# A post-LN decoder block with recurrent layers: other load order and other engines for the weight preparation ahead of the first step

## What is computed

```
for l in range(4):
    x = x + slstm(ln(x) * ln1_w[l], conv_w[l], conv_b[l], wi, wf, wz, wo, rker, cell_b, gn_w)[l]
    x = x + (gelu(u[..., :336]) * u[..., 336:]) @ ff_down[l],   u = ln(x) * ln2_w[l] @ ff_up[l]
x = ln(x) * post_w
```

## Time and profile before

| | us |
|---|---|
| median of 3 runs | 3654.46 (3654.07 to 3657.61) |
| profiled execution | 3654.35, its span 3652.6 |
| mean granted PE clock | 0.988 of full |
| PE / VectorE / ScalarE / GpSimd busy in the first 46 us | 11.0 / 33.4 / 1.3 / 1.6 |
| busy over the whole span, same order | 3518.5 / 3414.1 / 3045.7 / 2311.6 |

### The profile page before, as it was taken

The page is one execution under the profiler, slowest core; times in us unless marked ns, Lnnn a source line. Parts: engine busy times, 40 slices in busy tenths (PEclk is TensorE's granted clock), DMA queues, the critical chain, the costliest instruction groups (busy, mean ns, idle before and its releaser), DMA issues. The chain is left out here.

```text
span 3652.6 us, 168847 instructions
## 1 busy us (share of the span) xinstructions
PE 3518.5 (96%) x71457; PEld 2338.8 (64%) x71489; DVE 3414.1 (93%) x9400; ACT 3045.7 (83%) x6636; POOL 2311.6 (63%) x2515
## 2 busy tenths in 40 slices
PE   5999999999999999999999977999999999999997
PEld 3666666666666666666666654666666666666665
DVE  8999999999999999999999987999999999999997
ACT  4999999999999999999999965767776767777775
POOL 3777777777777777777777737555555555555552
PEclk9999999999999999999999998999999999999998
DMA  2000222000011010111001100000000000000000
GB/s 83 26 25 26 57 60 56 26 26 26 25 26 27 26 26 26 26 27 26 25 26 25 27 28 18 25 25 25 25 25 25 27 30 28 25 25 25 24 8 10
DMA packets 99980, 104.35 MB, mean 29 GB/s; under 512 B 17296, under 2 KB 95004, under 8 KB 98728
## 3 DMA queue, kind: packets, MB, share of 16 engines
q1 hardware_dynamic: 99224, 93.56, 9.0%
HBM read 48.52 MB, written 17.53 MB: 18 GB/s over the span
## 5 line engine op out<-in xcount | busy, mean ns | idle before, releaser
L572 POOL TENSOR_TENSOR conv_products<-normed_features,conv_taps_by_token 128x256 f32<-128x256 f32 (+1 forms) x837 | 758.2, 921 | 597.7 <-ACT normed_features L355 419.6
L299 PE MATMUL banks<-up_centred,after_cell_features 128*32 128x336 f32 x8928 | 684.2, 446 | 4.0 <-DVE after_cell L534 3.7
L783 POOL TENSOR_TENSOR exps_of_both_halves<-scores 128x256 f32<-128x256 f32 x512 | 404.5, 815 | 427.3 <-ACT scores L1062 424.8
L299 PEld LDWEIGHTS banks<-up_centred,after_cell_features 128*32 128x32 f32 x8928 | 302.2, 109 | 299.8 <-issue 245.6
L306 PE MATMUL banks<-down,hidden_features 112*32 112x256 f32 x6696 | 420.8, 383 | 0.2
L1062 ACT ACTIVATE scores<-scores 128x512 f32<-128x512 f32 x512 | 302.8, 624 | 81.4 <-DVE scores L1213 81.4
L394 ACT ACT_TABLE_LOAD x279 | 358.0, 1283 | 4.9
L373 ACT ACT_TABLE_LOAD x279 | 358.0, 1283 | 4.9
L585 POOL TENSOR_TENSOR conv_partial_sums<-conv_products,conv_partial_sums 128x512 f32<-128x512 f32 x279 | 358.4, 1284 | 0.0
L1213 DVE SCALAR_TENSOR_TENSOR scores<-banks,score_top 128x512 f32<-128x512 f32 x512 | 317.3, 681 | 6.4 <-PE banks L888 3.0
L273 PE MATMUL banks<-recurrent_weights,h_features 64*32 64x256 f32 x8928 | 313.8, 380 | 0.0
(11 more groups left out here) (224 smaller groups left out, 9946.5 us busy)
## 6 DMA issues: line engine op xcount, KB each, us to landing
layer_inputs<-layer_outputs SPq DMA_DIRECT2D x279, 96.0 KB, 2.1
layer_inputs<-in_x SPq DMA_DIRECT2D x280, 32.0 KB, 1.8
x_scratch<-layer_outputs SPq DMA_DIRECT2D x279, 32.0 KB, 2.1
x_tokens<-in_x SPq DMA_DIRECT2D x32, 256.0 KB, 3.1
context_features<-in_ctx SPq DMA_DIRECT2D x32, 256.0 KB, 3.7
layers_out<-x_scratch SPq DMA_DIRECT2D x32, 256.0 KB, 2.8
out<-result SPq DMA_DIRECT2D x64, 128.0 KB, 1.8
up_centred<-in_ff_up SPq DMA_DIRECT2D x1, 2688.0 KB
```

Of the source, the lines that this page charges most:

```text
L299: mm = nc.tensor.matmul(bank[group(l), b, 0:UP], xmt[:, n, group(l)], up[:, l, n, at:at + UP], start=n == 0, stop=n == HALF - 1, skip_grou ...
L572: return nc.gpsimd.tensor_tensor(prod[:, i:i + n], xnt[:, j % NRING].rearrange("p n t -> p (n t)")[:, None, :].broadcast_to([P, n, HALF * ...
L783: nc.gpsimd.tensor_tensor(psum[:, i % RING, :], pr[:, i % RING, 0:S], pr[:, i % RING, S:2 * S], ALU.add).then_inc(halves_added, 1)
```

## The change

- SP issues the bias rows first, then ln2, ln1, taps, conv bias and gn_w, then `up`, then gate and recurrent weights, then `down`. Each group has a semaphore: `rows_loaded`, `small_loaded` (5 loads), `up_loaded`, `gates_loaded` (2), `down_loaded`. PE waits for the last of these ahead of the down product of step 0.
- `up` is scaled by ScalarE, eight activations with the function Identity and a scale for each partition.
- PE waits for each layer's two scaled halves and signals the means of each layer; VectorE subtracts layer by layer.
- 14 of the memsets go to GpSimd, which signals `zeroed` after each (`CLEARED` = 14), and so do the ten fills of partial sums. `mean_w` is set first on VectorE.
- VectorE's order becomes: remaining memsets, bias, centre, taps and `gnc`, `bn_stats`, then the gate weights, then the subtraction.

```diff
         def _(sy):
-            for dst, src in ((wg, a["gate_w"]), (rk, a["rker"]), (up, a["ff_up"]), (down, a["ff_down"]), (conv_w, a["conv_w"]), (conv_b, a["conv_b"]),
-                             (ln1, a["ln1"]), (ln2, a["ln2"]), (gnc, a["gn_w"]), (rows, a["bias"])):
-                sy.dma_start(dst[:], src).then_inc(w_loaded, DMA)
+            sy.dma_start(rows[:], a["bias"]).then_inc(rows_loaded, DMA)
+            for dst, src in ((ln2, a["ln2"]), (ln1, a["ln1"]), (conv_w, a["conv_w"]), (conv_b, a["conv_b"]), (gnc, a["gn_w"])):
+                sy.dma_start(dst[:], src).then_inc(small_loaded, DMA)
+            sy.dma_start(up[:], a["ff_up"]).then_inc(up_loaded, DMA)
+            for dst, src in ((wg, a["gate_w"]), (rk, a["rker"])):
+                sy.dma_start(dst[:], src).then_inc(gates_loaded, DMA)
+            sy.dma_start(down[:], a["ff_down"]).then_inc(down_loaded, DMA)
             sy.wait_ge(zeroed, 1)
...
-            pe.wait_ge(w_step, UP_SCALED)
+            pe.wait_ge(mean_made, 1)
             for l in range(LAYERS):
+                pe.wait_ge(up_scaled, HALF * (l + 1))
                 for m in range(2):
                     for n in range(HALF):
...
-            mm.then_inc(up_means, 1)
+                mm.then_inc(up_means, 1)
...
+                if j == 0:
+                    pe.wait_ge(down_loaded, DMA)
                 feed_down().then_inc(down_done, 1)
...
+            act.wait_ge(small_loaded, SMALL * DMA)
+            act.wait_ge(up_loaded, DMA)
+            for l in range(LAYERS):
+                for m in range(HALF):
+                    nc.scalar.activation(up[:, l, m, :], up[:, l, m, :], ACT.Identity, scale=ln2[:, l, m:m + 1]).then_inc(up_scaled, 1)
             act.wait_ge(first_gates, 1)
...
+            nc.vector.memset(mean_w[:], 1.0 / D).then_inc(mean_made, 1)
             n = 0
-            for buf, val in ((xr, 0.0), (h, 0.0), (half_r, 0.0), (ls, NEVER), (dl, 0.0), (xm, 0.0), (xst, 0.0), (prod, 0.0), (hid, 0.0),
-                             (hidt, 0.0), (xnt, 0.0), (xmt, 0.0), (gl, 0.0), (xn, 0.0), (stat2, 0.0), (rstd, 0.0), (eps, EPS), (bias, 0.0), (pick16, 0.0),
-                             (mean_w, 1.0 / D), (begun, 0.25 * H_SCALE), (never, 0.0)):
+            for buf, val in ((bias, 0.0), (pick16, 0.0), (stat2, 0.0), (rstd, 0.0), (eps, EPS), (begun, 0.25 * H_SCALE), (never, 0.0)):
...
-            dve.wait_ge(w_loaded, DMA * LOADS)
...
+            dve.wait_ge(rows_loaded, DMA)
             f_ = rows[:, 0:1024].rearrange("p (h g d) -> p h g d", h=HEADS, g=GATES)[:, :, 1, :]
...
+            for r in (0, 64):
+                nc.vector.tensor_scalar(centre[r:r + DH, :], ident[r:r + DH, r:r + DH], -1.0 / DH, None, ALU.add).then_inc(w_step, 1)
+            dve.wait_ge(small_loaded, SMALL * DMA)
...
+            dve.wait_ge(zeroed, CLEARED)
+            nc.vector.bn_stats(stat2[:], xm[:, 0]).then_inc(w_step, 1)
+            n += 1
+            dve.wait_ge(gates_loaded, 2 * DMA)
             for l in range(LAYERS):
+                for m in range(HALF):
+                    w_ = wg[:, l, m, 2:4, :].rearrange("p g d -> p (g d)")
+                    nc.vector.tensor_scalar(w_, w_, ln1[:, l, m:m + 1], None, ALU.mult).then_inc(w_step, 1)
...
+            for l in range(LAYERS):
+                dve.wait_ge(up_means, l + 1)
                 for m in range(HALF):
                     w_ = up[:, l, m, :].rearrange("p (k n) -> p k n", k=2)
                     nc.vector.tensor_tensor(w_, w_, bank[:, 2 * l:2 * l + 2, 0:UP], ALU.subtract).then_inc(w_step, 1)
...
             dve.wait_ge(bias_made, 10)
+            dve.wait_ge(parts_made, 2 * (TAPS + 1))
             dve.sem_inc(w_ready, 1)
...
+            for buf, val in ((xr, 0.0), (xm, 0.0), (h, 0.0), (half_r, 0.0), (ls, NEVER), (dl, 0.0), (xst, 0.0), (prod, 0.0), (hid, 0.0),
+                             (hidt, 0.0), (xnt, 0.0), (xmt, 0.0), (gl, 0.0), (xn, 0.0)):
+                nc.gpsimd.memset(buf[:], val).then_inc(zeroed, 1)
+            pool.wait_ge(small_loaded, SMALL * DMA)
+            for turn_ in range(2):
+                for k in range(TAPS + 1):
+                    b_ = conv_b[:].rearrange("p l n -> p n l")
+                    nc.gpsimd.tensor_scalar(part[:, turn_, k].rearrange("p (n l b) -> p n l b", n=HALF, l=LAYERS),
+                                            b_[:, :, :, None].broadcast_to([P, HALF, LAYERS, B]), 0.5, None, ALU.mult).then_inc(parts_made, 1)
             pool.wait_ge(w_ready, 1)
```

More of the change, by code:

```diff
@@ L32 @@
 ROW_SCALE = 16.0
-UP_SCALED = 39
 EPS = 1e-5
@@ L222, in group @@
         return slice(32 * l, 32 * l + 32)
-    LOADS = 10
+    SMALL, CLEARED = 5, 14
     FIRST_PIECE = 40
@@ L420, in _ @@
-            dve.wait_ge(const_made, 4)
[L421 to L426, removed]
@@ L436, in _ @@
-            n += 1
-            for k in range(TAPS):
-                w_ = conv_w[:, :, :, TAPS - 1 - k].rearrange("p l n -> p n l")
-                nc.vector.tensor_copy(taps[:, k], w_[:, :, :, None].broadcast_to([P, HALF, LAYERS, B])).then_inc(w_step, 1)
-            for turn_ in range(2):
-                for k in range(TAPS + 1):
-                    b_ = conv_b[:].rearrange("p l n -> p n l")
-                    nc.vector.tensor_scalar(part[:, turn_, k].rearrange("p (n l b) -> p n l b", n=HALF, l=LAYERS),
-                                            b_[:, :, :, None].broadcast_to([P, HALF, LAYERS, B]), 0.5, None, ALU.mult).then_inc(w_step, 1)
@@ L457, in _ @@
             nc.vector.tensor_tensor(rows_lo[:], rows_rest[:], rows_mid[:], ALU.subtract).then_inc(bias_made, 1)
+            dve.wait_ge(w_step, n)
             nc.vector.tensor_scalar(bias[0:3 * LAYERS], rows_hi[:], part_of[:, 0:1], None, ALU.mult).then_inc(bias_made, 1)
@@ L465, in _ @@
             nc.vector.tensor_scalar(pick16[0:3 * LAYERS], pick[:], 1.0 / ROW_SCALE, None, ALU.mult).then_inc(bias_made, 1)
-            dve.wait_ge(up_means, 1)
-            for l in range(LAYERS):
+            for r in (0, 64):
+                nc.vector.tensor_scalar(centre[r:r + DH, :], ident[r:r + DH, r:r + DH], -1.0 / DH, None, ALU.add).then_inc(w_step, 1)
+            dve.wait_ge(small_loaded, SMALL * DMA)
+            nc.vector.scalar_tensor_tensor(out=conv_w[:], in0=conv_w[:], scalar=0.5, in1=ln1[:][:, :, :, None].broadcast_to(
+                [P, LAYERS, HALF, TAPS]), op0=ALU.mult, op1=ALU.mult).then_inc(w_step, 1)
+            n += 3
+            dve.wait_ge(w_step, n)
+            nc.vector.tensor_tensor(gnc[:].rearrange("p l n d -> p (l n) d"), gnc[:].rearrange("p l n d -> p (l n) d"),
+                                    centre[:, None, :].broadcast_to([P, LAYERS * HALF, DH]), ALU.mult).then_inc(w_step, 1)
+            for k in range(TAPS):
+                w_ = conv_w[:, :, :, TAPS - 1 - k].rearrange("p l n -> p n l")
+                nc.vector.tensor_copy(taps[:, k], w_[:, :, :, None].broadcast_to([P, HALF, LAYERS, B])).then_inc(w_step, 1)
+            n += TAPS + 1
+            dve.wait_ge(zeroed, CLEARED)
+            nc.vector.bn_stats(stat2[:], xm[:, 0]).then_inc(w_step, 1)
+            n += 1
+            dve.wait_ge(gates_loaded, 2 * DMA)
+            for l in range(LAYERS):
+                for m in range(HALF):
+                    w_ = wg[:, l, m, 2:4, :].rearrange("p g d -> p (g d)")
+                    nc.vector.tensor_scalar(w_, w_, ln1[:, l, m:m + 1], None, ALU.mult).then_inc(w_step, 1)
+            for w_ in (wg, rk):
+                f_ = w_[:].rearrange("p l h g d -> p (l h) g d")[:, :, 1, :]
+                nc.vector.tensor_scalar(f_, f_, -1.0, None, ALU.mult).then_inc(w_step, 1)
+            n += LAYERS * HALF + 2
+            for l in range(LAYERS):
+                dve.wait_ge(up_means, l + 1)
                 for m in range(HALF):
```

15 lines of the change are left out of this document (4 added, 11 removed).

## The result

The change takes 3639.68 us (median of 5 runs, 3638.77 to 3641.24) against 3654.46 before (5 runs, 3653.03 to 3657.61): ratio 0.9958, interval 0.9947 to 0.9969, so 14.8 us or 0.40% faster. The profiled execution took 3639.34 us, its span is 3637.6 (3652.6 before), its mean granted clock 0.989.

The account below looks back on a forecast made before the run. A long, almost all VectorE chain ahead of the first step was taken as the bound: PE's means end at 25.0, plus 1.6 and 1.35 gives 28.0 instead of 45.98, 18.0 us saved, so 3636.4 us; range 3632.5 to 3641.5.

Parts of the forecast that it names:

- the 93%: Whole kernel: the chance given to a measured time faster by more than the 7.3 us that a measurement can tell.
- the 28.0 of the sum: End of the front: first matmul of step 0 forecast at 28.0 us instead of 45.98, a gain of 18.0 us.
- the short form of the port rival: Front: some four GpSimd fills each delay a VectorE gate-weight operation, 3.0 us; start 29.9, time 3638.3; port rival's chance 15%.
- the long form: Front: VectorE's ten gate-weight operations lose 0.55 us each beside GpSimd's fills, 5.5 us; start 32.4, time 3640.8; rival's chance 15%.
- Loads: Front: loads served in issue order, small ones first, `up` loaded at 11.9 us, gate and recurrent weights 16.8, `down` 21.2.
- the 0.757 priced: Front, ScalarE: one scaling of `up` takes 757 ns, two for a layer 1.5 us, all eight 6.1 us.
- 11.0 to 12.2: Front, PE: range in us for the 32 matmuls of the means, started at 13.4; 11.6 taken, ending at 25.0.
- Free at 3.4, bias chain 7.4 us: 11.0: Front, VectorE: remaining clearing over at 3.4 us, bias rows loaded by then, bias chain done at 11.0.
- The 1.1 us of slack: Front: VectorE, unhindered, would reach the last layer's subtraction at 23.95, 1.1 us before PE ends at 25.0.
- the sign that I had given for the port rival: Front: no idle time of VectorE before the last subtraction would show that VectorE and GpSimd hinder each other; chance 15%.
- The rival (28%): Step 0: PE's clock survives the 3.0 us gap before it, saving 1.7 us more, time 3634.7; chance 28%.
- Slower: Loop: it falls out of step, with more waits for rows moved by DMA; 75 give 3665.6 us; chance 3%.

Follow-up runs that it names:

- e4: The kernel before with only the new order of loads and a semaphore for each group; 3651.07 us, one run, against 3661.84 for the kernel before on that chip.
- e3: The change with GpSimd's clears held back until VectorE has done its first three bias operations; 3639.53 us, one run, against 3661.84 for the kernel before there.
- c_before: The kernel before itself, unchanged, profiled once more; 3657.53 us over 11 runs, against 3657.58 over 15 runs beside it, ratio 0.9999.
- e8: The change with `up` loaded in four parts, clears on ScalarE, only fills on GpSimd, layers 0 to 2 subtracted early; 3640.01 us, ratio to before 0.9952.
- e7: The change with 14 unread matmuls on PE between the last mean and the first bias matmul; 3642.13 us, one run, against 3654.96 before on that chip.
- e10: The change with 14 unread matmuls before the first bias matmul and ten more while step 0's `h` is made; 3638.43 us, one run, against 3658.22 before.
- e5: The change with `up` scaled by VectorE again, ahead of the bias; 3644.47 us, one run, against 3654.96 for the kernel before on that chip.
- e9: The change with `up` in four loads, clears on ScalarE, early subtraction, and 26 unread matmuls first on PE; 3635.98 us, ratio to before 0.9941.

## Why the prediction was right, point by point

The time (3636.4 forecast, range 3632.5 to 3641.5) came out 3.3 us above the forecast and inside the range, faster as the 93% said. That is in part luck. The start of step 0 came at 30.12, 2.1 us after the 28.0 of the sum and nearly where the short form of the port rival put it (29.9), by another road; its times (3638.3, and 3640.8 in the long form) are nearer to the measured one than the forecast's. Of the 3.3 us, 1.7 are the front (16.3 gained up to the first activation instead of 18.0), 1.3 the scatter of loop and rest, the remainder the difference of medians and profiles.

- *Loads.* In order, as argued: e4 shows it, and gate weights landed at 18.0 in e3 (16.8 forecast). `up` landed at 12.7, not 11.9. The mis-sized term is its transfer: its packets ran from 5.07 to 12.32 us, 7.25 us where 6.5 were priced from 424 GB/s (6.9 us in before), at first beside those of `gn_w`, the last and largest of the small loads. Its start was 0.3 us late, and the landing came sooner behind the last packet than priced.
- *ScalarE.* Right in the sum: one every 0.76 us, worked out from the earlier trace rows; no load of a table appears between the load's landing and them. One operation lasts 0.84 us, longer than the 0.757 priced, but the next starts before it ends. The hand-over to PE cost 0.2 us that the sum lacked: 14.49, where 12.75 + 1.5 gives 14.25.
- *PE.* 12.18 us, the upper end of the range (11.6 taken). The slow stretch was 5.7 us, from 14.49 to 20.23, near the 5.9 of step 0. But its length is no property of the kernel: before had 3.5 us and 11.00 for the means, c_before, the same program, 5.2 and 11.89, and the other runs between 3.5 (e8, 11.00 us) and 6.1 (e3, 12.31); behind 26 others the means took 9.21. So 11.0 to 12.2 was the honest term, and where in it the change fell is chance. PE ended at 26.67, 1.7 late: 0.85 load, 0.25 hand-over, 0.6 clock.
- *VectorE.* This step failed. "Free at 3.4, bias chain 7.4 us: 11.0" took the bias rows as the only thing to wait for. (3.4 + 7.4 is 10.8; the slip ahead of a wait changes nothing.) The chain ended at 16.8: 6.0 us in the first operation, the rest in one-input operations stretched beside the fills (0.41 for 0.21, 0.60 for 0.47). I had named this very contention and put it at the gate weights, where it cost 0.35 us; it belonged where GpSimd's row of clears meets VectorE's first one-input operation. The 5.8 us of lateness ate the idle time in front of the gate weights and left the subtraction to start at 22.58 instead of 19.3. The 1.1 us of slack was gone, and no pause stood before the last layer: the sign that I had given for the port rival.
- *GpSimd.* Clears done at 9.1, the lower end. The fills took 1.28 us each instead of 0.75, ended at 21.84 and were, as costed, due later.
- *What the miss is made of.* PE's lateness alone gives 29.7, as e3 shows at 29.72; VectorE adds the last 0.4. The large miss on VectorE cost little, because PE was late by nearly as much; that the two coincide is luck.
- *Clock.* It fell, as the forecast took as given, but 3.9 us after the last matmul and not 2.7 (in c_before it was 3.6, so this too differs between runs of one program): the first bias matmuls still ran at 2.4 GHz (0.64 us for 1.06). Step 0 took 9.70 us. The rival (28%) was priced wrongly: e7 and e10 show that surviving this gap alone gives nothing and surviving both 0.6 us, not 1.7.
- *Slower.* The loop is 1.75 us longer, by chance, as c_before shows: the mean step is 7.5215 us against 7.5152. Of the 16.3 us that the front gave, 1.3 went there and in the rest together.

## What to carry to other kernels

Before moving work to another engine, price what the engine that is left will meet on the shared port: fourteen clears and ten fills moved from VectorE to GpSimd freed 8.6 us on paper and 0.9 in the runs, while eight scalings moved to ScalarE freed 3.9 on paper and 8.4 against e5 (some 5 by the estimate above, had VectorE's order been better), since an engine with nothing else to do can wait in everybody's place. Issue first what the longest chain starts with, and split it so that the chain can start on its first part (e8: first mean at 8.4 instead of 14.5). Judge an edit of the front by an instant that repeats, and know the spread of the whole before believing a few microseconds of it.

## What the runs showed of the hardware that was not expected

- A one-input VectorE operation with 256 elements on 12 partitions stood for 6.30 us behind fourteen GpSimd clears issued back to back, the first of them under way, and one with 1024 for 6.34; in e3 two others got in after the end of one clear and the whole of the next, and stretched the clear behind from 0.30 to 0.86 and from 0.37 to 0.65 us. Two-input VectorE operations beside clears kept their 1.21 us.
- GpSimd's fill (one input, 128x256, a broadcast operand) took 1.28 us beside a busy VectorE, 0.89 in e3, where VectorE idled for part of it; VectorE's own takes 0.21.
- The granted clock fell 2.7 us after PE's last matmul in before, 3.6 in c_before, the same program, 3.9 in the change and 2.7 to 4.1 in the others where it fell around the start of step 0; and in e7 some 2.0 us into a gap of 2.54 us, when PE had worked for 1.0 us since a gap of 0.92. It rose 3.5 us after the first of the means in before, 5.2 in c_before, and 3.5 to 6.1 in the others (e9 aside, where 26 matmuls ran ahead of them).
- Four small loads of 28 KB in all, issued 0.4 to 0.5 us apart behind the bias rows, moved 14 GB/s over two microseconds with the DMA engines 16% busy; in the 8.5 us behind them the traffic was 388 GB/s.
- Up to 163.1 and as little as 158.9 us went by between the last step's first activation and the first store of the output, with the same instructions and the granted clock low in other places.
